# Attention heads: the four query tiles of a head-step taken from the longest to the shortest

## The reference

```
scores = einsum(query, key) * scale         # 512 x 512 of each head
scores = where(causal, scores, -1e9)
attn   = softmax(scores)
out    = einsum(attn, value) @ W_o
```

## Time and profile before

| | before |
|---|---|
| median of 3 runs | 1889.4 us (1888.31 to 1897.15) |
| span of the profiled execution | 1890.7 us |
| heads stage, 223 to 1196 us | 973 us |
| busy in the span: PE / DVE / ACT / POOL | 79% / 73% / 56% / 51% |
| granted TensorE clock in the heads stage | 0.99 of full speed |

### The profile page before, as it was taken

One profiled execution on the slowest core, in us unless ns is written; L12 is line 12 of the kernel. 1 busy time (PEld: TensorE's weight loads), 2 busy tenths in 40 slices (PEclk: granted clock), 3 DMA queues, 4 the chain that ended last, 5 costly groups with the idle time before them and its releaser, 6 DMA issues. The chain is left out here.

```text
span 1890.7 us, 38527 instructions
## 1 busy us (share of the span) xinstructions
PE 1502.3 (79%) x10367; PEld 1317.0 (70%) x10369; DVE 1389.6 (73%) x3895; ACT 1054.1 (56%) x2993; POOL 963.3 (51%) x1154
## 2 busy tenths in 40 slices
PE   2762399889988899898898999587999999897551
PEld 2652378778877787787787788466888888786541
DVE  2895298978879889888898889364555577676665
ACT  1330177766767677676676677354666666565100
POOL 1120187767767778777777778300000034444686
PEclk8666599999999999999999999877999999998665
DMA  3993511141221111111111111185545577686664
GB/s 145 342 371 115 224 52 57 38 147 54 100 95 46 56 57 38 61 62 55 50 48 58 54 46 35 60 268 168 162 152 162 160 223 224 202 245 197 197 201 130
DMA packets 169557, 243.66 MB, mean 129 GB/s; under 512 B 16786, under 2 KB 139666, under 8 KB 165010
## 3 DMA queue, kind: packets, MB, share of 16 engines
q1 hardware_dynamic: 146322, 186.76, 29.7%
q0 software_dynamic: 18432, 50.36, 8.6%
q10 hardware_dynamic: 4608, 4.20, 0.8%
HBM read 117.52 MB, written 123.73 MB: 128 GB/s over the span
## 5 line engine op out<-in xcount | busy, mean ns | idle before, releaser
L982 ACT ACTIVATE prob<-ps,negmax 128x128 f32<-128x128 f32 (+3 forms) x512 | 270.2, 528 | 242.1 <-DVE negmax L1057 239.9
L1057 DVE TENSOR_REDUCE negmax<-ps 128x1 f32<-128x128 f32 (+3 forms) x512 | 248.3, 485 | 63.3 <-PE ps L898 61.4
L56 PE MATMUL ps<-kt_hi,qt_hi 128*128 (+4 forms) x512 | 200.4, 391 | 98.9 <-ACT prob L982 79.6
L818 POOL TENSOR_TENSOR prob<-prob,rinv 128x384 f32<-128x384 f32 (+1 forms) x256 | 238.9, 933 | 20.1
L831 POOL DMA_INDIRECT sorted_x<-xn_row,row_no x192 | 190.9, 994 | 49.6 <-issue 49.3
L1072 DVE TENSOR_TENSOR pt_lo<-ps,pt_hi 128x512 fp32r<-128x512 f32 (+1 forms) x256 | 207.1, 809 | 1.5 <-ACT pt_hi L988 1.5
L988 ACT ACTIVATE pt_hi<-ps 128x512 fp32r<-128x512 f32 (+1 forms) x256 | 166.5, 703 | 36.6 <-PE ps L909 35.7
L56 PEld LDWEIGHTS ps<-kt_hi,qt_hi 128*128 128x128 f32 x512 | 100.0, 195 | 119.7 <-ACT prob L982 98.3
L815 POOL TENSOR_TENSOR rinv<-rowsum,minus_one 128x1 f32<-128x1 f32 x256 | 146.7, 573 | 69.7 <-ACT prob L982 68.3
L909 PE MATMUL ps<-ident,prob 128*128 128x128 f32 x1280 | 168.8, 276 | 8.0 <-POOL prob L818 8.0
L923 PE MATMUL ps<-pt_hi,nkv 128*128 128x512 f32 (+3 forms) x512 | 164.1, 331 | 4.6 <-DVE pt_lo L1072 4.6
(11 more groups left out here) (246 smaller groups left out, 4992.2 us busy)
## 6 DMA issues: line engine op xcount, KB each, us to landing
sorted_x<-zeros SPq DMA_DIRECT2D x16, 2048.0 KB, 9.6
rows_in<-sorted_x SPq DMA_DIRECT2D x128, 256.0 KB, 2.8
sorted_y<-rows_out SPq DMA_DIRECT2D x128, 256.0 KB
nqt<-nqt_dram SPq DMA_DIRECT2D x16, 512.0 KB, 4.2
raw_gu<-in_wgu SPq DMA_DIRECT2D x16, 384.0 KB, 4.0
x_in<-in_x SPq DMA_DIRECT2D x8, 512.0 KB, 4.3
xn_dram<-xn SPq DMA_DIRECT2D x8, 512.0 KB, 5.1
xnt_dram<-xnt_hi SPq DMA_DIRECT2D x16, 256.0 KB, 4.7
```

Source lines behind the costliest of these rows:

```text
L56: pe.matmul(out, lh, rh, start=first, stop=False, **kw)
L818: pool.tensor_tensor(prob[:, i, qt, 0:w], prob[:, i, qt, 0:w], rinv[:, i, qt:qt + 1].to_broadcast([P, w]), ALU.mult).then_inc(normed_pool, 1)
L982: act.activation(prob[:, i, qt, 0:w], s_ps[qt % 2][:, 0:w], ACT.Exp, bias=negmax[:, i, qt:qt + 1], accum_out=rowsum[:, i, qt:qt + 1]).then ...
L1057: dve.tensor_reduce(negmax[:, i, qt:qt + 1], s_ps[qt % 2][:, 0:(qt + 1) * P], AX.X, ALU.max, negate=True).then_inc(max_ready, 1)
```

## The change

A list `Q_ORDER = [3, 2, 1, 0]` gives the order of the query tiles, `unit` counts by it, and the lists of all engines follow it: where a step had tiles 0, 1, 2 and 3 of scores, maxima and exponentials at its four places, it now has 3, 2, 1 and 0. The banks alternate as before. GpSimd keeps tiles 2 and 3, but scales tile 3 at the end of its own step and tile 2 at the start of the next one (before: 2, then 3). VectorE keeps tiles 0 and 1, but scales tile 1 behind the queries of its own step, and tile 0 only in the next step, behind its first maximum (before: both behind the queries). `turn` takes the tiles in the order 3, 2, 1, 0. On ScalarE the exponentials of tiles 0, 1, 2 and 3 become those of 3, 2, 1 and 0 at the same four places of its step. No operation is added, removed or resized. The core of the diff:

```
+Q_ORDER = [3, 2, 1, 0]
...
-    def unit(b, g, qt=0):
-        return TT * (NH * b + g) + qt
+    def unit(b, g, qt=Q_ORDER[0]):
+        return TT * (NH * b + g) + Q_ORDER.index(qt)
@@ GpSimd, step
                 if bt.back(g, 1):
-                    norm(*bt.back(g, 1), TT - 1)
+                    norm(*bt.back(g, 1), 2)
...
                 if g < NH:
-                    norm(bt.now, g, 2)
+                    norm(bt.now, g, 3)
@@ TensorE, turn
-                for qt in range(TT):
-                    pe.wait_ge((normed_dve, normed_pool)[qt // 2], 2 * (NH * b + g) + qt % 2 + 1)
+                for qt in Q_ORDER:
+                    pe.wait_ge((normed_dve, normed_pool)[qt // 2], 2 * (NH * b + g) + 2 - qt % 2)
@@ TensorE, step
-                    scores(bt.now, g, 0)
+                    scores(bt.now, g, 3)
                 if par == 0 and bt.next_pair(p):
                     queries(*bt.next_pair(p), 4 * todo[0] + 2 * todo[1] + todo[2] + 1 if todo else None)
                 if par == 1 and bt.next_pair(p):
                     queries_turn(*bt.next_pair(p))
                 if g < NH:
+                    scores(bt.now, g, 2)
                     scores(bt.now, g, 1)
-                    scores(bt.now, g, 2)
                 if bt.back(g, 2):
                     values(*bt.back(g, 2))
                 if bt.back(g, 1):
                     turn(*bt.back(g, 1))
                 if g < NH:
-                    scores(bt.now, g, 3)
+                    scores(bt.now, g, 0)
@@ VectorE, step
                 if now:
-                    maxima(bt.now, g, 0)
+                    maxima(bt.now, g, 3)
+                if bt.back(g, 1):
+                    norm(*bt.back(g, 1), 0)
                 if bt.back(g, 2):
                     turned_lo(*bt.back(g, 2), 1)
                 if now:
+                    maxima(bt.now, g, 2)
                     maxima(bt.now, g, 1)
-                    maxima(bt.now, g, 2)
...
                 if now:
-                    norm(bt.now, g, 0)
                     norm(bt.now, g, 1)
                 if bt.back(g, 2):
                     latent_add(*bt.back(g, 2))
                 if now:
-                    maxima(bt.now, g, 3)
+                    maxima(bt.now, g, 0)
                 if bt.back(g, 1):
                     turned_lo(*bt.back(g, 1), 0)
```

More of the change, by code:

```diff
@@ L816, in norm @@
                     .then_inc(rinv_pool, 1)
-                pool.wait_ge(rinv_pool, 2 * (NH * b + g) + qt - 1)
+                pool.wait_ge(rinv_pool, 2 * (NH * b + g) + TT - qt)
                 pool.tensor_tensor(prob[:, i, qt, 0:w], prob[:, i, qt, 0:w],
@@ L887, in scores @@
             def scores(b, g, qt):
-                if qt == 0:
+                if qt == Q_ORDER[0]:
                     pe.wait_ge(qt_lo, NH * b + g + 1)
@@ L894, in scores @@
                 w = (qt + 1) * P
-                s = s_ps[qt % 2]
+                s = s_ps[Q_ORDER.index(qt) % 2]
                 product3(pe, s[:, 0:w], [a[:, qt * P:w] for a in qt_s[g // 2 % 2][g % 2]],
@@ L981, in exps @@
                 act.wait_ge(max_ready, unit(b, g, qt) + 1)
-                act.activation(prob[:, i, qt, 0:w], s_ps[qt % 2][:, 0:w], ACT.Exp, bias=negmax[:, i, qt:qt + 1],
+                act.activation(prob[:, i, qt, 0:w], s_ps[Q_ORDER.index(qt) % 2][:, 0:w], ACT.Exp, bias=negmax[:, i, qt:qt + 1],
                                accum_out=rowsum[:, i, qt:qt + 1]).then_inc(exp_done, 1)
@@ L1009, in step @@
                 if g < NH:
-                    exps(bt.now, g, 0)
+                    exps(bt.now, g, 3)
                 if nxt:
@@ L1016, in step @@
                 if g < NH:
-                    exps(bt.now, g, 1)
+                    exps(bt.now, g, 2)
                 if nxt and par == 1:
@@ L1020, in step @@
                 if g < NH:
-                    exps(bt.now, g, 2)
+                    exps(bt.now, g, 1)
                 if bt.back(g, 2):
@@ L1029, in step @@
                 if g < NH:
-                    exps(bt.now, g, 3)
+                    exps(bt.now, g, 0)
             queries_latent(0, 0)
@@ L1056, in maxima @@
                 dve.wait_ge(s_ready, unit(b, g, qt) + 1)
-                dve.tensor_reduce(negmax[:, i, qt:qt + 1], s_ps[qt % 2][:, 0:(qt + 1) * P], AX.X, ALU.max,
+                dve.tensor_reduce(negmax[:, i, qt:qt + 1], s_ps[Q_ORDER.index(qt) % 2][:, 0:(qt + 1) * P], AX.X, ALU.max,
                                   negate=True).then_inc(max_ready, 1)
@@ L1064, in norm @@
                 dve.reciprocal(rinv[:, i, qt:qt + 1], rowsum[:, i, qt:qt + 1]).then_inc(rinv_dve, 1)
-                dve.wait_ge(rinv_dve, 2 * (NH * b + g) + qt + 1)
+                dve.wait_ge(rinv_dve, 2 * (NH * b + g) + 2 - qt)
                 dve.tensor_scalar(prob[:, i, qt, 0:w], prob[:, i, qt, 0:w], rinv[:, i, qt:qt + 1], None, ALU.mult)\
```

## The result

The changed kernel takes 1921.6 us (median of 4 runs, 1921.1 to 1923.1), beside 1888.9 for the kernel before (4 runs, 1885.3 to 1897.2): ratio 1.0161, interval 1.0133 to 1.0189. The forecast was 1918. In the profiled execution the span is 1921.2 and the time of that same run 1923.05.

The account below looks back on a forecast made before the run. VectorE, with a blocked scaling, was taken to pace pairs without a piece, TensorE those with one. Per batch 1.8 + 0.5 + 1.1 + 0.5 = 3.9 us, times 7.75 gives 30; forecast 1918 us, range 1867 to 1928.

Parts of the forecast that it names:

- step (4): VectorE's tile-0 scaling in odd steps, starting 0.04 us ahead of GpSimd's 384-wide multiplication, is held, 0.66 us late; chance 0.50.
- R: Start of GpSimd's rope addition in the even step, from which the prediction counts all times in a pair of head-steps.
- The second delay: VectorE's next tile-0 scaling, made late by the first hold, is held by GpSimd's 512-wide multiplication and loses 0.4 us.
- the first rival: VectorE wins the 0.04 us in the odd step, its scaling is unhindered: pair 13.3 us, kernel 1873 us; chance 0.33.
- Steps (1) and (2): TensorE's wait at the second score block shrinks from 0.7-1.4 to about 0.1 us; odd steps' third block newly idles about 0.85.
- Step (3): VectorE's second low part of the turned queries comes 0.35 us later, while its 0.5 us wait for scores goes.
- The pair: Two head-steps without a piece of the output projection: 13.3 us plus holds of 0.66 and 0.4, so 14.35 us.
- Three pairs: Heads stage, from one piece's residual addition over three pairs: 45.25 us after against 43.46 before, +1.8.
- Pair with a piece: Pair of head-steps beginning with a piece of the output projection: 16.55 us after against 16.08 before, +0.5.
- the seam: The triple of pairs holding the loop's seam, where all engines stop, was counted at +1.1 us.

Follow-up runs that it names:

- e1: Changed kernel plus one spare 128x1 GpSimd multiplication ahead of tile 2's reciprocal in odd steps; 1871.3 us, ratio 0.9908 to the kernel before.
- e10: e1 plus two spare 128x1 VectorE copies ahead of tile 0's reciprocal in odd steps; ratio 1.0186 to the kernel before.
- e2: Changed kernel with VectorE's scaling of the previous step's tile 0 ahead of the 512-wide maximum instead of behind it; ratio 1.0173 to the kernel before.
- e4: Kernel before (ascending order) with both VectorE scalings moved behind the latent addition, tile 3's maximum and the 512 low parts; ratio 1.0129 to the kernel before.
- e9: e1 plus one spare 128x1 VectorE copy ahead of tile 0's reciprocal in odd steps; ratio 0.9881 to the kernel before.
- e5: Kernel before plus the same spare 128x1 GpSimd multiplication as e1 in every odd step; ratio 0.9999 to the kernel before.
- e7: Changed kernel with tile 1's scaling behind the latent addition and tile 0's maximum in even steps only; ratio 0.9782 to the kernel before, repeated 0.9776.
- e3: Changed kernel with tile 1's scaling moved behind the latent addition, tile 0's maximum and the 512 low parts; ratio 1.0217 to the kernel before.

## Why the prediction was right

**The walk and the choice in step (4).** VectorE's scaling was forecast at R+3.54 and the multiplication at R+3.58; they came at R+3.52 and R+3.54, and the choice, held for 0.66, is what the trace shows (0.93 against 0.29: 0.64). The second delay was put at 0.4; the even step's scaling takes 0.56 to 0.63, so 0.3. That this choice carries the sign is shown by e1: the same order with a larger lead gives the first rival's time within 2 us. The choice itself was little better than a toss, at 0.50 against 0.33. Its reason was that some forgotten delay would put VectorE behind; none did, VectorE starts 0.01 to 0.03 us ahead in every odd step from 300 to 1150 us, and it is held all the same, since a lead of 0.04 loses too (e10). Right outcome, and in that point another reason than the one given.

**Steps (1) and (2).** The wait at the second block is down to 0.1 or 0.2 us where it occurs, that of the third block is 0.66 where 0.85 was forecast; the total fell from 70.5 to 39.8. I called them nearly cancelling; e2 and e4 show that this holds only for as long as nothing is put ahead of the maximum they hang on.

**Step (3)** was an estimate of 0.35 and measured 0.30, 54 times between 300 and 1150 us.

**The pair** was forecast at 14.35 and takes 14.15 and 14.30. That looks closer than it is. The walk of step (3) started from 13.46, the window of the earlier trace rows, but from R to R the pair before took 13.82 (718.09 to 731.91 in the earlier trace rows). So the pair grew by 0.35 to 0.5, where the walk added 0.89: a base too short and costs too large partly cancel. What the choice of step (4) is worth, 14.35 less 13.3, was right: 14.15 to 14.30 against 13.15 to 13.2 in e1. Three pairs: +1.43 (forecast +1.8). Pair with a piece: +0.35 (+0.5).

**The mis-sized term is the seam.** I counted +1.1 for the triple that holds the loop's seam. There are six such triples. In the first two it is +0.7 and +1.3, in the last four +2.2 to +2.7. TensorE at one of the last four seams and its window over the twelve query products that follow, before:

```profile
895.55 0.32 PE L56 MATMUL ps<-kt_hi,qt_hi 128*128 x1 [1.49 <-issue]
```

```profile
895.50:897.60 2.10, 2.05 (x17) 2.06 (x18) 0.69 (x2) 0.55 (x2) 2.00 (x3) 1.00 0.42 140
```

and after:

```profile
911.38 0.50 PE L58 MATMUL ps<-kt_hi,qt_hi 128*128 x1 [2.49 <-issue]
```

```profile
912.20:915.00 2.80, 2.80 (x15) 2.80 (x15) 2.26 (x5) 0.78 (x2) 0.82 (x1) 0.50 0.18 53
```

TensorE now has only the 128-wide block at the end of the step before, and stands idle at the seam for 2.49 instead of 1.49 us; behind that its granted clock is 0.50, the 1.2 GHz level, and the twelve products take 2.71 us (912.28 to 914.99) instead of 1.51 at the full clock (896.02 to 897.53). These 1.2 us are about the size that I missed. An idle of 2.5 to 2.8 and twelve slow products stand at each of the four seams from 650 to 1050 us, where it was 1.3 to 1.5 and full clock before. At the first two seams the idle is 5.4 to 6.2 us and the granted clock over the products 0.50 in both kernels, so nothing is added by the clock there, and those triples grew less.

What the lower clock is worth can be read in e9, where it comes at one of the last four seams and not at the other three. The window over the twelve products behind an idle of 2.32 us, and behind one of 2.33 three batches later:

```profile
646.73:649.38 2.65, 2.65 (x12) 2.13 (x11) 1.63 (x5) 0.77 (x2) 2.21 (x3) 0.50 0.18 54
1006.06:1007.66 1.60, 1.60 (x14) 1.32 (x13) 0.79 (x3) 0.00 (x0) 1.52 (x3) 1.00 0.07 21
```

The triple around the first takes 46.28 us, the other three 45.14 to 45.18. So some 1.1 us go with the lower clock in the descending order. In e5, in ascending order, it is only some 0.4: 0.50 follows idles of 1.89 and 1.82 us at two of the last four seams, and these triples take 46.58 and 46.75 against 46.11 and 46.41. The two seams of e9 also show that the length of the idle does not settle it, as 2.32 was followed by 0.50 and 2.33 was not. So that the shorter block makes the longer idle, and the longer idle the lower clock, is argued from the order of the rows and not shown; no run took either away.

Between the first and the last residual addition lie six seam triples, eight other triples and fifteen single pairs (the last two distances do not change): 11.7 + 8 x 1.43 + 15 x 0.35 = 28.4 us, where the terms of the forecast give 6 x 1.1 + 8 x 1.8 + 15 x 0.5 = 28.5. The seams are 5 us too small in it and the other terms 5 us too large. That 1921.6 came so close to 1918 is therefore in part luck.

**What bounds the pair.** The prediction said that VectorE sets the pace in a pair without a piece. e4 contradicts that as a rule: with 66 us less of scaling there between 300 and 1150 us, the 32 additions took 18 us longer. It is the place of VectorE's time that counts, not its sum.

**The Trainium skill's rule.** The prediction set a rule against its own choice: the Trainium skill (SBUF — State Buffer, Who interferes with whom) gives the shared ports to whichever engine issues first. By recorded starts the rule holds where VectorE is behind (718.11 of the earlier trace rows) and where it leads by 0.06 or more (e5, e9, e1, e7). It fails at leads up to 0.05 (the changed kernel, e10, three steps of e5), where VectorE starts first and is held for all of GpSimd's operation. Whether the recorded start of one engine is later or earlier than its claim on the ports, no run here separates.

## What to carry to other kernels

Where two engines' operations can hold one another, walk both lists to the hundredth from a common point. In these traces every lead up to 0.05 us was lost and every one from 0.06 up was won, and a walk is good to some 0.04, so count on a lead only from about 0.1. If it decides, a tiny instruction that computes nothing (e1), or another slot (e7), can be worth more than the reordering itself. Place a scaling that can be held where the other engine does something small and no maximum that TensorE waits for stands behind it: freeing the engine in the wrong slot (e2, e3, e4) gained nothing. And walk the loop's seam by itself, with the clock.

## What the runs showed that I had not expected

- An instruction of 0.19 us that computes nothing made the changed kernel 48 us faster, by the ratios.
- By the recorded starts a lead of 0.04 us loses and one of 0.10 wins (e10, e9), in every odd step from 300 to 1150 us; over all traces the limit lies between 0.05 and 0.06, without an exception.
- GpSimd's 128x1 reciprocals do not hold a scaling: in e2 one of 0.28 us at 717.73 lies wholly beside a reciprocal of 0.55 at 717.70.
- At the seam of an otherwise full stage an idle of 2.49 us was followed by 0.50 of the clock and one of 1.49 was not; but in e9 one of 2.32 was and one of 2.33 was not, and in e5 one of 1.89 was.
